# Turning the next batch's rows behind the scores in steps 4 to 7 of an attention and mixture-of-experts kernel

## The reference

```python
xn = _layernorm(x, axis=-1)                      # x: (8, 512, 512)
qkv = x @ Wqkv.T + b_qkv                         # attention, x stands for xn here
scores = jnp.einsum('bqhd,bkhd->bhqk', q, k) * scale + bias   # bias falls with distance, by head
p = jax.nn.softmax(jnp.where(causal, scores, -1e9), axis=-1)
ctx = jnp.einsum('bhqk,bkhd->bqhd', p, v).reshape(B, S, D)
s = ctx @ Wout.T + b_out
h = jnp.einsum('nd,ehd->enh', xn, w_fc); a = jnp.square(jnp.where(h >= 0, h, 0.5 * h))
g = _silu(out_of_the_expert_with_the_larger_logit * its_probability)
x = x + s * g
```

## Time and profile before

| | |
|---|---|
| Time, median of 3 runs | 1419.25 us (1418.3 to 1422.16) |
| Time of the profiled execution | 1421.55 us |
| Its span, first to last instruction | 1419.8 us |
| Mean granted clock of PE | 0.991 |
| Iterations b = 1 to 6, each | 82.7 us |

### The profile page before, as it was taken

The page is one execution under the profiler, slowest core; times in us unless marked ns, Lnnn a source line. Parts: engine busy times, 40 slices in busy tenths (PEclk is TensorE's granted clock), DMA queues, the critical chain, the costliest instruction groups (busy, mean ns, idle before and its releaser), DMA issues.

```text
span 1419.8 us, 30098 instructions
## 1 busy us (share of the span) xinstructions
PE 1362.1 (96%) x9761; PEld 870.8 (61%) x9761; DVE 932.5 (66%) x2456; ACT 777.4 (55%) x1835; POOL 689.9 (49%) x894
## 2 busy tenths in 40 slices
PE   4889999999999999999799999999999999999997
PEld 2455555656555565655466666666666666666665
DVE  7678778778777877877789745555445555544444
ACT  3588778787877878787756422322323222232222
POOL 1466666666566656656533344443334433334333
PEclk9999999999999999999899999999999999999999
DMA  4525344343534434345266321221112121112110
GB/s 175 162 71 179 106 130 140 110 143 94 175 110 138 131 118 133 96 144 144 87 222 215 106 58 56 57 61 38 37 57 54 51 59 53 39 44 57 48 34 30
DMA packets 119458, 140.56 MB, mean 99 GB/s; under 512 B 48655, under 2 KB 97807, under 8 KB 117136
## 3 DMA queue, kind: packets, MB, share of 16 engines
q1 hardware_dynamic: 110368, 112.81, 26.3%
q0 software_dynamic: 8944, 25.83, 5.7%
HBM read 97.81 MB, written 33.95 MB: 93 GB/s over the span
## 4 chain that ended last, share of the span: by engine, by line
PE 82%; DVE 7%; POOL 4%; ACT 3%; issue 2%; DMA 1%; SPq 0%; DVEq 0%; POOLq 0%; ACTq 0%
PE psF L1255 23%; PE psY L1275 23%; PE psA L368 20%; PE psT L469 7%; PE psA L484 5%; PE psS L448 3%; POOL pr L1057 2%; DVE pr L967 1%; PE psA L432 1%; POOL pre L1074 1%; DVE xT L858 1%; DMA pt<-in_wqkv 1%; ACT pr L624 1%; ACT xT L582 1%; ACT cf L573 1%
## 5 line engine op out<-in xcount | busy, mean ns | idle before, releaser
L1255 PE MATMUL psF<-xT,wf 128*128 128x256 f16 (+1 forms) x3264 | 368.0, 269 | 0.0
L1275 PE MATMUL psY<-wf,aT 128*128 x1584 | 363.9, 379 | 0.4 <-DVE aT L1435 0.4
L1255 PEld LDWEIGHTS psF<-xT,wf 128*128 x3264 | 312.0, 98 | 63.6
L1509 POOL TENSOR_TENSOR a<-a 128x512 f32<-128x512 f32 (+1 forms) x136 | 156.0, 1147 | 370.1 <-DVE a L1426 369.6
L1057 POOL TENSOR_SCALAR pr<-pr,rden 128x128 f32<-128x128 f32 (+3 forms) x512 | 265.1, 536 | 139.3 <-DVE rden L978 137.9
L624 ACT ACTIVATE pr<-pr,mn 128x128 f32<-128x128 f32 (+3 forms) x512 | 282.1, 554 | 0.3 <-DVE mn L967 0.3
L967 DVE CUSTOM_DVE_ANT_0 pr<-psS,base,nsl 128x128 f32<-128x128 f32 (+3 forms) x512 | 250.2, 544 | 3.1 <-PE psS L448 2.8
L1275 PEld LDWEIGHTS psY<-wf,aT 128*128 128x128 f16 x1584 | 154.5, 98 | 158.9 <-issue 1.1
L469 PE MATMUL psT<-conf,pr 128*128 128x128 f32 x1280 | 205.2, 279 | 4.7 <-POOL pr L1057 3.0
L1340 ACT ACTIVATE rl<-psF 128x512 f32<-128x512 f32 (+1 forms) x136 | 79.3, 583 | 220.6 <-PE psF L1255 217.0
L469 PEld LDWEIGHTS psT<-conf,pr 128*128 128x128 f32 x1280 | 159.3, 143 | 65.6 <-POOL pr L1057 12.7
(11 more groups left out here) (176 smaller groups left out, 1299.9 us busy)
## 6 DMA issues: line engine op xcount, KB each, us to landing
qk_parts<-pre SPq DMA_DIRECT2D x64, 256.0 KB, 2.8
qs<-qk_parts SPq DMA_DIRECT2D x128, 128.0 KB, 2.7
ks<-qk_parts SPq DMA_DIRECT2D x128, 128.0 KB, 2.7
wst<-in_wf SPq DMA_DIRECT2D x16, 1024.0 KB, 5.2
wstage<-in_wf SPq DMA_DIRECT2D x32, 512.0 KB, 4.7
xin<-in_x SPq DMA_DIRECT2D x32, 256.0 KB, 4.2
attn_out<-so SPq DMA_DIRECT2D x32, 256.0 KB, 2.0
xT<-wstage SPq DMA_TRANSPOSE x216, 2.3
```

Source lines behind the costliest of these rows:

```text
L1255: last = nc.tensor.matmul(psF[c % 2][:, k * TT:k * TT + tn], w(e, 2 * hc, hl, kc * 512 + col, P), xT[:, r % 2, x, kc, 0:tn], start=(m == 0 ...
L1275: last = nc.tensor.matmul(psY[r % 2][h][:], aT[:, c % 4, x, k, h * P:(h + 1) * P], w(e, 2 * hc + 1, hl, q * 512, 512), start=(c == 0 and k ...
L1509: nc.gpsimd.tensor_tensor(at, at, at, ALU.mult).then_inc(s["a_ready"], 1)
```

## The change

In steps 4 to 7 of iterations 0 to 6, the x job is taken out of its place among the jobs, and done behind the scores, before P times V.

```diff
--- before.py
+++ after.py
@@ -491,6 +491,8 @@
                 g, j = step // HG, step % HG
                 ptrans(b, g, j, 0)
                 todo = [p for p in STEP[step] if job_exists(b, p) and JOBS[p][0] != "ctx"]
+                late = [p for p in todo if b >= 0 and JOBS[p][0] == "x"]
+                todo = [p for p in todo if p not in late]
 
                 def between():
                     ptrans(b, g, j, 1)
@@ -510,6 +512,8 @@
                 hb, h = head_at(b, step + S_LEAD)
                 if within(hb, 0, B):
                     scores(hb, h)
+                for p in late:
+                    job(b, odd, p, lambda: None)
 
                 for p in STEP[step]:
                     if JOBS[p][0] == "ctx" and job_exists(b, p):
```

## The result

The changed kernel takes 1442.93 us in the median (1440.89 to 1447.29, 4 runs) against 1420.7 for the kernel before (1418.3 to 1423.28, 4 runs): a ratio of 1.0154, 95% interval 1.0138 to 1.017. The profiled execution took 1440.89 us with a span of 1439.1; the one of before 1421.55 and 1419.8.

A forecast was written before the change was run, and what follows sets the result against it. PE, busy 96% of the span, was taken as the bound. Six batches at 3.45 - 1.12 + 0.70 = 3.03 us (18.2) plus 3.0 for batch 0 gave 21.2 us more: 1440.5 us, range 1432 to 1449 (8 in 10).

The forecast's parts named there:

- The handover: Output products of steps 6 and 7 and q in step 8 each wait 1.15 us behind a turning: 3.45 per batch.
- the loop: Batch 0: PE, ACT, DVE without cover, 5.05 us a round, 22.0 us from DVE's step 4 to step 8.
- The removed waits: Third turning no longer waits for rows (0.74 us) and q's old wait (0.38) goes: 1.12 us saved per batch.
- The late mask: Step 6: DVE runs 0.76 us late, so the last score waits for the last mask, 0.7 us per batch.
- Step 4 costs nothing: First turning, step 4: P times V behind it uses another bank and DVE has idle time, so no loss.
- Batch 0: First batch, without output products to cover the waits: 2.6 us slower plus 0.4 for the clock, 3.0 us.
- the allowance: Batch 0: 0.4 us added for score and turning while the clock is granted at 0.50.
- Two handovers only: Rival: only the output products' waits on the turning's own bank cost, q's is hidden; 14.3 us, 1433.5 us, chance 0.07.
- Faster: Rival: handovers are short enough, under 1.23 us, leaving only the removed waits; some 8 us gained, 1411 us, chance 0.06.
- Absorbed: Rival: other engines are ahead of a delayed PE afterwards, so no change; within 4 us of 1419, chance 0.05.
- Clock in every batch: Rival: waits bring PE to 1.2 GHz in every batch, 7 to 14 us more, 1448 to 1455 us, chance 0.10.
- a granted clock under 1.00 after 100 us: Sign in the next profile that would show the forecast wrong: PE's clock lowered later than 100 us.

The follow-up runs named there:

- o2 first, search early: Kernel before, third turning (x job) and third output product exchanged in the job table, DVE's weight search ahead of the read-outs: 1416.46 us, ratio 0.9963.
- only step 5 late: Kernel before with only the turning (x job) of step 5 moved behind the scores: 1424.2 us, ratio 1.0017.
- banks exchanged: Changed kernel with the third turning (x job) and third output product exchanged in the job table, so also their banks: 1436.99 us, ratio 1.0109.
- only step 7 late: Kernel before with only the turning (x job) of step 7 moved behind the scores: 1425.32 us, ratio 1.002.

## Why the prediction was right

**Direction and size.** Forecast were 1440.5 us and +1.5%; measured are 1442.93 and +1.54%. The batch was forecast to grow by 3.03 us and grew by 2.93. The part on batches 1 to 6 is right term by term. That the whole came so close is partly luck: by the profiled spans the forecast of 18.2 + 3.0 = 21.2 us stands against 17.5 + 3.7 - 1.9 = 19.3, and the 1.9 us behind the last batch's first output product were not foreseen.

**The handover, 3 x 1.15.** Right in place and size: 2.01 to 2.02 us from start to start, three times a batch, as in the earlier trace rows. Its share is not a plain sum, though: with the output products moved to the other bank a batch gained only 0.86 us of the 2.3 that the two bank waits have on paper, because the loop through DVE takes nearly the same time. The forecast of the total needs both; the sentence that each of three places costs 1.15 us on its own needs this correction.

**The removed waits, 1.12.** Right. No wait for rows is left, and "o2 first, search early" shows 0.78 us for the 0.74 alone.

**The late mask, 0.7.** Right: 0.66 by the starts, 0.65 by taking the search out of its way. The mechanism is DVE's 0.76 us of lateness; "only step 5 late" shows that lateness apart, there through the third turning's rows (+0.73).

**Step 4 costs nothing.** Right, -0.04.

**Batch 0, 3.0.** Mis-sized: from step 4 to step 8, DVE took 101.84 - 77.80 = 24.04 us where 22.0 (22.4 with the allowance) was reckoned and 19.38 was the time before. DVE's timeline of the changed kernel:

```profile
77.80 0.17 DVE L982 RECIPROCAL rden<-den 128x4 f32<-128x4 f32 x1
...
101.84 0.17 DVE L982 RECIPROCAL rden<-den 128x4 f32<-128x4 f32 x1
```

The term that was missing in this execution is the clock on P times V. PE's timeline and the window there:

```profile
80.63 4.04 PE L484 MATMUL psA<-pt,v 128*32 128x512 f32 x32
84.60 1.31 PE L469 MATMUL psT<-conf,pr 128*128 128x128 f32 x10
```

```profile
80.00:84.00 4.00, 4.00 (x25) 1.44 (x28) 2.63 (x9) 1.30 (x3) 2.30 (x5) 0.58 0.48 137
```

P times V takes 3.97 us from start to start, where the same 32 matmuls take 2.29 in later batches, and the granted clock was 0.58 on average from 80 to 84 us, so at 1.2 GHz most of that time and not at 2.4. PE had waited for the masks in the two microseconds before and was busy 0.78 of them. I had allowed 0.4 us for the clock, where this product alone lost 1.7.

The kernel with the banks exchanged has the same order on PE in its first batch, and serves as a control. PE's P times V there, and DVE's step 4 and step 8:

```profile
79.38 2.36 PE L484 MATMUL psA<-pt,v 128*32 128x512 f32 x32
```

```profile
76.54 0.17 DVE L982 RECIPROCAL rden<-den 128x4 f32<-128x4 f32 x1
...
98.90 0.17 DVE L982 RECIPROCAL rden<-den 128x4 f32<-128x4 f32 x1
```

P times V runs at full clock, and DVE takes 22.36 us: the 22.4 that was reckoned, and 1.68 less than in the changed kernel's trace. So the loop was sized well, and the miss is the clock. The single rounds fit less well: 4.97, 6.87, 5.67 and 4.85 us, where 5.05, 6.49, 5.05 and 5.38 were reckoned; in the second, ACT reads the turning 1.09 us after its start and not 0.63, being still busy with the context and the exponentials, which the walk left out. The slow P times V (4.0 us) stands in four of the five traces in which the turning of step 4 is late, and in none of the other eight (2.36). It is thus tied to the change but not certain: the control had the same waits for the masks ahead of it (1.46 and 0.33 us, against 1.46 and 0.34), and kept its clock. What decides is not shown.

At batch 1's first output product the error is smaller, 3.7 us against 3.0. This execution came to step 4 0.5 us earlier than the one before, and took 0.5 less from q to that output product.

**The rivals.** *Two handovers only*: refuted by "only step 7 late", which loses 0.73 us at q. *Faster*: its point of decision was a handover of 1.23 us, and it is 2.01. *Absorbed*: the batch grew by nearly the whole sum, and none of it came back in steps 9 to 15: from q to the next batch's first output product it is 60.45 us before (263.91 to 324.36) and 60.43 after (273.46 to 333.89). *Clock in every batch*: 1.00 over the whole batch, and from 102 to 676 us altogether; of the changed places only batch 0 lost by it. The sign "a granted clock under 1.00 after 100 us" does occur in iteration 7, but in the kernel before as well: 30 to 50 us behind the last batch's first output product the clock is 0.83 and 0.69 in two stretches of 10 us before, and 0.83 and 0.83 after. That is up to 1.4 us of PE's time and may be most of the 1.9 us; it is not shown to be the cause. The Trainium skill (Perfetto Trace Analysis, "Optimizing Tensor Performance", Matmuls) advises rotation of banks; the runs agree that it helps (85.62 to 84.76), and show that here the greater part of the wait stays for another reason.

## What to carry to other kernels

Before you move work to the end of a step, ask what the next step starts with: an in-order engine needs at least the length of the read-out chain (2.01 us here) of other work between a producer and the first instruction that needs its result or its bank. Freeing a bank gains little where a loop through another engine is nearly as long; take both away, or reckon the loop's full round against the work in a step. And look for the delay's other half on the reader: work of DVE that nobody waits for (the weight search) was best put where DVE waited anyway. A table that is good in the middle can cost at the ends, where the work that lay between two uses of a bank is missing: read the first and the last iterations by themselves.

## What was not expected of the hardware

A waiting PE can pay twice, and need not. After the waits of batch 0, P times V ran at a granted clock of 0.58 and took 1.7 us more in four of five traces; in the fifth it ran at 1.00 behind waits of the same length. In the kernel before, moving only DVE's search ahead of the read-outs removed a stretch at 0.50 and took 0.29% off the time, although the batches in the middle did not change; the low clock had cost PE 1.3 us in that stretch, which is a part of it at most.
